# Attention distances: queries and their squares stacked on 128 rows, one product per head in column halves

## What is computed

```python
q, k, v = h @ Wq, h @ Wk, h @ Wv          # 8 heads of 64
k0, k1 = k - mu[0], k - mu[1]
d0 = -scale / 2.0 * sqdist(q, k0)         # sqdist = q.q + k.k - 2 q.k
d1 = -1.5 * scale * sqdist(q, k1)
prob = softmax(maximum(d0, d1), over the keys)
out = layernorm(h + (prob @ v) @ Wo)
```

## Time and profile before

| | |
|---|---|
| median of 3 runs | 2453.52 us (2449.77 to 2454.09) |
| profiled execution | 2452.1 us, span 2450.3 us |
| mean granted TensorE clock | 0.941 |
| attention stage in the trace | first work at 1489.3 us, last at 2054.5 us |

### The profile page before, as it was taken

How to read it: one execution, slowest core, us unless ns; L and a number is a source line. 1 busy time by engine, 2 the same in 40 slices (tenths; PEclk the granted TensorE clock), 3 DMA queues, 4 the chain that set the end, 5 groups by cost and what they waited for, 6 DMA issues and landing times. The chain is left out here.

```text
span 2450.3 us, 41718 instructions
## 1 busy us (share of the span) xinstructions
PE 2134.8 (87%) x14183; PEld 1496.8 (61%) x14183; DVE 1588.2 (65%) x3564; ACT 1230.3 (50%) x2063; POOL 915.0 (37%) x763
## 2 busy tenths in 40 slices
PE   5799999979998599999999997999999995776671
PEld 4567868855555466666666664777777774555450
DVE  4432333346777588888888875676767664666673
ACT  2334464344554367677667675555655562332330
POOL 0000000013443378777778772000000001786772
PEclk9999999989999699999999999999999996678995
DMA  7660010019920100000000000000000001214554
GB/s 262 245 245 18 27 34 11 1 43 419 420 117 2 69 1 1 0 0 0 0 0 0 0 1 20 1 0 0 0 0 0 0 1 45 83 43 122 165 154 154
DMA packets 64688, 165.46 MB, mean 68 GB/s; under 512 B 12310, under 2 KB 43460, under 8 KB 55084
## 3 DMA queue, kind: packets, MB, share of 16 engines
q1 hardware_dynamic: 51564, 148.42, 17.0%
q0 software_dynamic: 7104, 12.71, 1.5%
q10 hardware_dynamic: 5888, 2.62, 0.4%
HBM read 68.81 MB, written 96.86 MB: 68 GB/s over the span
## 5 line engine op out<-in xcount | busy, mean ns | idle before, releaser
L1261 POOL TENSOR_TENSOR c_both<-c_hid 128x512 f32<-128x512 f32 x384 | 491.6, 1287 | 144.5 <-ACT c_hid L1234 106.2
L1234 ACT ACTIVATE c_hid<-c_scaled,c_b 128x1024 f32<-128x1024 f32 x384 | 437.1, 1150 | 172.9 <-DVE c_scaled L1308 158.0
L1308 DVE TENSOR_TENSOR c_scaled<-c_p_h,c_shares 128x1024 f32<-128x1024 f32 x384 | 454.5, 1215 | 80.5 <-PE c_p_h L1177 79.5
L1182 PE MATMUL c_p_o<-c_both,c_w 128*128 128x512 f32 x768 | 390.8, 591 | 0.0
L1175 PE MATMUL c_p_h<-c_x_hi,c_w_hi 128*128 128x512 f32 x384 | 291.9, 760 | 2.6 <-DVE c_w_lo L1331 2.6
L624 POOL TENSOR_TENSOR d_ln_rstd<-d_ln_var,d_ln_power 128x2 f32<-128x2 f32 x48 | 33.4, 696 | 525.3 <-DVE d_ln_var L620 525.3
L240 POOL COPY a_work<-a_vec 128x64 f32<-128x64 f32 x4 | 1.2, 303 | 444.4 <-PE a_p_A L322 256.0
L1182 PEld LDWEIGHTS c_p_o<-c_both,c_w 128*128 128x128 f32 x768 | 144.3, 188 | 36.1 <-issue 2.2
L1176 PE MATMUL c_p_h<-c_x_lo,c_w_hi 128*128 128x512 f32 x384 | 152.6, 397 | 0.0
L1492 PEld LDWEIGHTS d_p_s<-d_kk,d_q_bd 128*128 128x128 f32 x768 | 123.9, 192 | 45.9 <-issue 45.9
L1177 PE MATMUL c_p_h<-c_x_hi,c_w_lo 128*128 128x512 f32 x384 | 151.9, 396 | 0.0
(11 more groups left out here) (331 smaller groups left out, 4658.6 us busy)
## 6 DMA issues: line engine op xcount, KB each, us to landing
slots<-b_blank SPq DMA_DIRECT2D x56, 1040.0 KB, 23.7
band_scratch<-a_work SPq DMA_DIRECT2D x16, 1024.0 KB, 5.7
a_work<-band_scratch SPq DMA_DIRECT2D x16, 1023.5 KB, 7.9
e_wb<-e_weights SPq DMA_DIRECT2D x63, 164.0 KB, 2.5
a_raw<-in_Wc SPq DMA_DIRECT2D x16, 512.0 KB, 3.6
e_xb<-slots SPq DMA_DIRECT2D x63, 130.0 KB, 2.2
e_yb<-e_again SPq DMA_DIRECT2D x12, 512.0 KB, 5.6
a_work<-in_x_tok SPq DMA_DIRECT2D x16, 256.0 KB, 8.2
```

The source lines that it names most:

```text
L1182: nc.tensor.matmul(p_o[s][:, 0:N], w2[:, q, :], both[q % SLOTS][:, :], start=(q == 0), stop=(q == NQ - 1)).then_inc(s_down, 1)
L1234: nc.scalar.activation(hid[q % SLOTS][:, :, :], scaled[q % SLOTS][:, :, :], ACT.Gelu, bias=b1[:, q:q + 1]).then_inc(s_ge, 1)
L1261: nc.gpsimd.tensor_tensor(both[q % SLOTS][:, :], hid[q % SLOTS][:, 0, :], hid[q % SLOTS][:, 1, :], ALU.add).then_inc(s_bo, 1)
L1308: v.tensor_tensor(scaled[q % SLOTS][:, :, :], p_h[q % SLOTS][:, 0:N].unsqueeze(1).to_broadcast([128, 2, N]), shares[s][:, :, :], ALU.mult) ...
```

## The change

- `q_bd`, `q_sq` and `q_rows` go. A new `q_two` has 128 rows per head: the head's 64 query rows on its own half and their squares on the other half.
- `kk` becomes `k_two`, per head: the head's keys (both kinds) on its own half, and on the other half the constants -0.5 and -1.5, written once by VectorE (`halves`).
- In `scores`, one product per head (128 rows in, 64 queries out) takes the place of two per head pair. Head `a` writes rows 64a to 64a+63 of `p_s`, so the two heads of a pair use the two column halves of the array. The product with `neg_half` stays.
- ScalarE's `queries` copies and squares each head from PSUM (four operations of 64 rows). A new ScalarE `keys` makes the keys of head 1 (two biased Identities, 64 rows) and both kinds of key squares from PSUM (two biased Squares, 128 rows, after a wait for VectorE's `keys`). `key_squares` goes.
- VectorE's `keys` makes only head 0's, on 64 rows. It takes over the second of the two value copies.
- The key projections wait for ScalarE's squares (`s_ksq`) where they waited for VectorE's keys (`s_k`).
- At the start GpSimd clears nothing, VectorE writes the constants and scaled means, and there are seven constant loads where there were eight.

The core of the diff:

```diff
@@ scores
-                pe.wait_ge(s_ksq, NT * g + t + 1)
-                pe.wait_ge(s_qsq, NHP * (g + 1))
+                pe.wait_ge(s_ksq, NHP * (g + 1))
+                pe.wait_ge(s_q, NHP * (g + 1))
+                if not exists(g - 2):
+                    pe.wait_ge(s_half, 2 * KINDS * (s + 1))
...
                     for hp in range(NHP):
-                        o = p_s[:, b, hp * 128:(hp + 1) * 128]
-                        nc.tensor.matmul(o, q_bd[s][:, hp, p, :], kk[s][:, p, hp, :, :].rearrange("p k j -> p (k j)"),
-                                         start=False, stop=False, skip_group_check=True)
-                        last = nc.tensor.matmul(o, q_sq[s][:, hp, p, :], q_rows[:, :], start=False, stop=hp == NHP - 1,
-                                                skip_group_check=True)
+                        for a in range(2):
+                            last = nc.tensor.matmul(p_s[64 * a:64 * a + 64, b, hp * 128:(hp + 1) * 128],
+                                                    q_two[s][:, hp, p, a, :],
+                                                    k_two[s][:, p, hp, a, :, :].rearrange("p k j -> p (k j)"),
+                                                    start=False, stop=hp == NHP - 1, skip_group_check=True)
@@ project and values
-                    pe.wait_ge(s_q if i % 2 == 0 else s_k, NHP * g + hp)
+                    pe.wait_ge(s_q if i % 2 == 0 else s_ksq, NHP * g + hp)
...
-                    pe.wait_ge(s_q if t == 0 else s_k, NHP * (g + 1))
+                    pe.wait_ge(s_q if t == 0 else s_ksq, NHP * (g + 1))
@@ ScalarE, queries and keys
                 for a in range(2):
-                    rows = slice(64 * a, 64 * a + 64)
-                    last = nc.scalar.copy(q_bd[s][rows, hp, :, 64 * a:64 * a + 64], by_position(p_p[0][rows, 0:M]))
+                    rows, other = slice(64 * a, 64 * a + 64), slice(64 - 64 * a, 128 - 64 * a)
+                    src = by_position(p_p[0][rows, 0:M])
+                    nc.scalar.copy(q_two[s][rows, hp, :, a, :], src)
+                    last = nc.scalar.activation(q_two[s][other, hp, :, a, :], src, ACT.Square)
                 last.then_inc(s_q, 1)
-                act.wait_ge(s_q, NHP * g + hp + 1)
-                nc.scalar.activation(q_sq[s][:, hp, :, :], q_bd[s][:, hp, :, :], ACT.Square).then_inc(s_qsq, 1)
...
+            def keys(g, s, hp):
+
+                if hp == 0 and exists(g - 2):
+                    act.wait_ge(s_s, NT * (g - 1))
+                act.wait_ge(s_proj, 10 * g + 2 * hp + 2)
                 for k in range(KINDS):
...
+                    nc.scalar.activation(k_two[s][64:128, :, hp, 1, k, :], by_position(p_p[1][64:128, 0:M]), ACT.Identity,
+                                         bias=mu_key[64:128, k, hp:hp + 1], scale=(1.0, 3.0)[k])
+                act.wait_ge(s_k, NHP * g + hp + 1)
+                for k in range(KINDS):
+                    last = nc.scalar.activation(k_sq[s][:, :, hp, k, :], by_position(p_p[1][:, 0:M]), ACT.Square,
+                                                bias=mu_sq[:, k, hp:hp + 1], scale=(1.0, 3.0 ** 0.5)[k])
                 last.then_inc(s_ksq, 1)
@@ ScalarE, values_out
-                for t in range(NT):
-                    act.wait_ge(s_proj, 10 * g + 9 + t)
-                    nc.scalar.copy(val[s][:, t, :], p_p[t][:, :]).then_inc(s_v, 1)
+                act.wait_ge(s_proj, 10 * g + 9)
+                nc.scalar.copy(val[s][:, 0, :], p_p[0][:, :]).then_inc(s_v, 1)
@@ ScalarE, body
                 def query(hp):
                     if ahead:
                         queries(g + 1, 1 - s, hp)
+                        keys(g + 1, 1 - s, hp)
@@ VectorE, keys and values_out
-                src = by_position(p_p[1][:, 0:M])
-                v.tensor_scalar(kk[s][:, :, hp, 0, :], src, mu[:, 0, hp:hp + 1], None, ALU.subtract)
-                v.tensor_scalar(kk[s][:, :, hp, 1, :], src, mu[:, 1, hp:hp + 1], 3.0, ALU.subtract, ALU.mult)\
+                src = by_position(p_p[1][0:64, 0:M])
+                v.tensor_scalar(k_two[s][0:64, :, hp, 0, 0, :], src, mu[0:64, 0, hp:hp + 1], None, ALU.subtract)
+                v.tensor_scalar(k_two[s][0:64, :, hp, 0, 1, :], src, mu[0:64, 1, hp:hp + 1], 3.0, ALU.subtract, ALU.mult)\
                     .then_inc(s_k, 1)
+
+            def values_out(g, s):
+                if exists(g - 2):
+                    dve.wait_ge(s_pv, NT * (g - 1))
+                dve.wait_ge(s_proj, 10 * g + 10)
+                v.tensor_copy(val[s][:, 1, :], p_p[1][:, :]).then_inc(s_v, 1)
@@ VectorE, body and start
                 if here:
                     probabilities(g, 1)
+                if ahead:
+                    values_out(g + 1, 1 - s)
                 if last:
                     ln2.statistics(dve, g - 1)
...
+            halves(0)
             dve.wait_ge(s_const, CONST)
+            v.tensor_scalar(mu_key[:, 0, :], mu[:, 0, :], -1.0, None, ALU.mult)
...
             for hp in range(NHP):
                 keys(0, 0, hp)
+            halves(1)
+            values_out(0, 0)
```

More of the change, by code:

```diff
@@ L1391, in phase_attention @@
         neg_half = sb("neg_half", [128, 128])
[L1392 removed]
+        mu_key = sb("mu_key", [128, KINDS, NHP])
+        mu_sq = sb("mu_sq", [128, KINDS, NHP])
         x_res = [sb(f"x_res{i}", [128, M]) for i in range(2)]
[L1395 to L1397 removed]
+        q_two = [sb(f"q_two{i}", [128, NHP, PB, 2, 64]) for i in range(2)]
+        k_two = [sb(f"k_two{i}", [128, PB, NHP, 2, KINDS, 64]) for i in range(2)]
         k_sq = [sb(f"k_sq{i}", [128, PB, NHP, KINDS, 64]) for i in range(2)]
@@ L1669, in body @@
                 query(3)
-                if ahead:
-                    key_squares(g + 1, 1 - s, 0)
                 if here:
@@ L1678, in body @@
                     vec_out(g, 0)
-                if ahead:
-                    key_squares(g + 1, 1 - s, 1)
-            act.wait_ge(s_set, 4)
             copy_x(0)
+            act.wait_ge(s_mu, 2)
             for hp in range(NHP):
                 queries(0, 0, hp)
-            for t in range(NT):
-                key_squares(0, 0, t)
+                keys(0, 0, hp)
             values_out(0, 0)
@@ L1694, in _ @@
             nc.gpsimd.memset(ln2.power[:, :], -0.5).then_inc(s_set, 1)
-            for q in q_bd:
-                nc.gpsimd.memset(q[:, :, :, :], 0.0).then_inc(s_set, 1)
-            pool.wait_ge(s_set, 4)
+            pool.wait_ge(s_set, 2)
             ln1.inverse_root(pool, 0)
@@ L1815, in body, with halves @@
                     ln2.normalise(dve, g - 1)
+            def halves(s):
+                for a in range(2):
+                    for k in range(KINDS):
+                        v.memset(k_two[s][64 - 64 * a:128 - 64 * a, :, :, a, k, :].rearrange("p b h j -> p (b h) j"),
+                                 (-0.5, -1.5)[k]).then_inc(s_half, 1)
             ln1.copy_in(dve, 0, columns(0), by_position)
```

20 lines of the change are left out of this document (6 added, 14 removed).

## The result

The changed kernel takes 2503.7 us (median of 4 runs, 2502.8 to 2505.7), beside 2453.3 us for the kernel before on the same chip: 1.0209 of it, with a 95% interval from 1.0194 to 1.0224. That is +50.4 us; the forecast was +41.5 (2495, range 2473 to 2522).

A forecast was written before the change was run, and what follows sets the result against it. TensorE was taken to bound the attention loop, with VectorE close behind. The new loop over three engines adds 22 x 1.57 = 34.5 us, start and end 7: 2453.5 + 41.5 = 2495, range 2473 to 2522.

The forecast's parts named there:

- rival A: TensorE's column halves run in turn, as the skill's weight-load rule would give: loop 25.4 us, 2525 in all; chance 0.06.
- Block and way back: On TensorE, one position's scores at 1.90 us, then 0.20 for returning to whole-array products.
- Rival C: TensorE stays the bound and its 2.3 us saving shows: 2441 to 2450 us; chance 0.05 faster.
- leg 4: ScalarE, from pair 0's Squares through `vec_out`, `exp`, pair 1's queries and keys to pair 2's key projection: 5.61 us.
- The ring: One attention step from pair 2's key projection to the next, over TensorE, VectorE and ScalarE: 24.04 us against 22.47.
- 1 project to output, residual: TensorE, from pair 2's key projection through one block, two projections, `norm_rows` and `output`: 5.84 us.
- 2 residual to distances: VectorE, from `residual` to ready for `distances`: 8.86 us today plus 0.61 for the added value copy, 9.47.
- 3 distances, shift, key: VectorE, `distances`, `shift` and the keys of pair 0: 3.12 us.
- rival B: TensorE's clock drops in the attention loop because of stalls, adding 0.4 to 0.8 us a step: 2504 to 2513; chance 0.12.
- its own +7: Attention stage's start and end: +6.2 to the first score product, +2 at step 1's layer norm, last step 1 shorter.
- a loop of 23.5 us: Low case for ScalarE's unknown prices: every such operation overlaps by 0.1 and bias is free; +27 in all, 2480.
- one of 24.9: High case for ScalarE's unknown prices: each such operation costs 0.05 to 0.1 more; +63 in all, 2516.

The follow-up runs named there:

- e1: Changed kernel with the score products issued head by head, all four pairs of one column half, then the other: ratio to the kernel before 1.0163.
- e4_fill: Changed kernel with four unread 128x256 products added on TensorE ahead of the key projection of pair 1: ratio to the kernel before 1.0126.
- e7: Changed kernel with the eight memsets of the constant halves on GpSimd instead of VectorE: ratio to the kernel before 1.0183.
- e2_key_early: Changed kernel with VectorE making the keys of pair 0 ahead of `shift(g, 0)`, not behind it: ratio to the kernel before 1.0010.
- e11_pool_alone: Changed kernel with only the key squares moved from ScalarE to GpSimd, with a second weight tile: ratio to the kernel before 1.0004.
- e5: Changed kernel with ScalarE's Squares of pair 0 moved behind `vec_out` and `exp(g, 0)`: ratio to the kernel before 1.0208.
- e10_pool_fixed: Changed kernel with key squares on GpSimd, squares products grouped per tile, both value copies on ScalarE: 2482.9 us beside 2517.9 for the kernel before.

## Why the prediction was right, and where it fell short

Its sign, its mechanism and most of its size held; it was 9 us short. That it came so close is in part luck, as two errors of opposite sign stand in the sum: the loop at full clock was put 6 to 7 us too long, and some 15 us of clock were left out. One of its own signs of being wrong came true, a granted clock under 0.95 from 1530 on: it was 0.92.

**The halves at once**: right. Sixteen records took 0.93 us without the tail against 0.89 forecast, and 1.42 with the heads in turn (e1). The rule beside rival A (the Trainium skill, "TensorE: Matmul & The Clock Gate", Part 3) doesn't hold for column halves here: by it no order of the heads could matter. Block and way back were forecast at 2.10 and took 2.01.

**ScalarE's prices**: right to 0.01 us each. Its lines and VectorE's, after (count, busy us, mean ns, idle):

```profile
L1612 ACT ACTIVATE d_k_sq<-d_p_p,d_mu_sq 128x256 f32<-128x256 f32 x154 | 64.7, 471 | 34.4 <-DVE d_k_two L1727 33.9
L1608 ACT ACTIVATE d_k_two<-d_p_p,d_mu_key 64x256 f32<-64x256 f32 x154 | 64.0, 463 | 1.9
L1599 ACT ACTIVATE d_q_two<-d_p_p 64x256 f32<-64x256 f32 x153 | 58.0, 379 | 1.8
L1598 ACT COPY d_q_two<-d_p_p 64x256 f32<-64x256 f32 x152 | 55.5, 365 | 11.8 <-PE d_p_p L1473 10.9
L1734 DVE COPY d_val<-d_p_p 128x512 f32<-128x512 f32 x19 | 13.0, 682 | 0.0
```

That is 0.47, 0.46, 0.38, 0.37 and 0.68 against 0.48, 0.473, 0.384, 0.367 and 0.693. The spacing of the four query operations is that of the earlier trace rows, with no overlap (1811.18, 1811.56, 1811.94, 1812.32). Rival C died here: the ten operations of leg 4 take 3.95 us, 0.40 each, not 0.26.

**The ring, leg by leg.** The changed kernel's legs, and those of e4_fill, which is the changed kernel at full clock:

| leg | forecast | e4 (clock 1.00) | changed kernel |
|---|---|---|---|
| 1 project to output, residual | 5.84 | 5.80 | 6.17 |
| 2 residual to distances | 9.47 | 9.45 | 9.45 |
| 3 distances, shift, key | 3.12 | 3.12 | 3.12 |
| 4 Squares to project | 5.61 | 5.41 | 5.55 |
| sum | 24.04 | 23.78 | 24.29 |

At full clock three legs are right to 0.04 and the fourth was put 0.20 too long: Squares and `vec_out` overlap what follows them and take 0.76 (1815.02 to 1815.75, and the wait ahead) and 0.51 in place of 0.90 and 0.56. So the working was good for 22 x 1.30 = 28.6 us of the loop and claimed 34.5 (e4's steps 1 to 22 take 521.2 us for 494.1, 27.1 more). With that and its own +7, the sum at full clock would have been 2489, 15 us under the measured time.

**The clock: the term that was missing.** The sum was made at full clock, and the clock stood aside as rival B with a chance of 0.12, on the ground that "work right after the stall has 1.5 us of slack". That ground didn't hold. The slack was the stall forecast before the projection of pair 2, 1.5 us (1.28 in e4); at the lower level the way from the key projection of pair 1 to the next query projection takes 4.04 us (1815.91 to 1819.95) where e4 takes 2.51 (1810.67 to 1813.18), 1.53 more. The slack is used up, leg 4 grows by 0.14, and the query bank of pair 2 comes late, for which ScalarE then waits 0.40 us; that returns as the 0.38 before the key projection of pair 3, in leg 1. With every sixth step at 25.5 the clock costs 0.67 a step, some 15 us in all: the price rival B was given (0.4 to 0.8). It wasn't a rival to the forecast but a part of it, since e4 shows that the stall before pair 1's key, forecast at 2.8 us in every step, is what brings it. The 2504 to 2513 of rival B came from adding that price to the loop's 34.5; the measured 2503.7 lies between 2495 and that.

**The predicted stalls**: 2.46 us before pair 1's key (2.8 forecast), ScalarE idle 1.46 (over 1), relu waiting 1.5 (under 2.0), `distances(g, 0)` not waiting: all seen. The stall before pair 2's key isn't there after, and is in e4: the lower clock hid it.

**The start.** ScalarE's longer list: +6.2 forecast, +6.4 measured, but not by its parts: ScalarE began 0.3 us later (1.3 forecast) and then took 14.2 us (13 forecast) for 8.1. Step 0 was put at +2 and came to +5.5. The memsets were sized right (0.91 each, 0.9 forecast), but e7 shows only 2.6 of it to be theirs, over steps 0 and 1. The cause of the rest isn't shown. It isn't mainly the ring, as e2_key_early, with the ring shortened, still has 26.5 us there for 27.2, while e11_pool_alone, with the memsets where they were and the Squares off ScalarE, has 21.4: that points at ScalarE's Squares. The tail was 1.9 shorter, 1 forecast. Together +10.0 for +7.

**Two bounds that don't add up.** By its own terms a loop of 23.5 us gives 22 x 1.03 + 7 = +30, not +27, and one of 24.9 gives +60, not +63. Neither moves the forecast.

## What to carry to other kernels

When a change takes work off the bound engine, draw the ring that the new waits close and add up its legs over all engines before counting the saving; here TensorE's shorter blocks (2.01 us for 2.65, 2.6 us a step) were real and worth nothing, since the Squares were put between a key bank and its release. A stall that such a sum forecasts on TensorE should be followed by a second sum with the work behind it at the lower clock. And where two ways run side by side, an edit that gives nothing isn't yet an edit without value: e5 gave nothing alone (24.46 us for 24.44) and 1.06 with the other way shortened.

## What the runs showed of the hardware that I hadn't expected

Useless products can be worth their time: 4 x 128x256 a step in a stall lifted the granted clock from 0.92 to 1.00 and took 0.67 us off a step of 24.4.

GpSimd's squares and some of VectorE's operations don't run side by side. `store_h` adds in SBUF; by tile, duration in ns (least, median, most), first in the changed kernel, then in e10_pool_fixed:

```profile
L1785 DVE TENSOR_TENSOR hT<-d_y,hT x18: 634/658/673, 1575.0 to 1991.2; 128x256 f32 x18
```

```profile
L1820 DVE TENSOR_TENSOR hT<-d_y,hT x21: 1206/1236/1283, 1566.2 to 1983.9; 128x256 f32 x20, 128x256 f32<-128x256 f32 x1
L1784 DVE TENSOR_SCALAR d_d_low<-d_d_min x48: 170/172/659, 1519.8 to 2005.3; 128x8 f32<-128x8 f32 x48
L1722 POOL TENSOR_TENSOR d_k_sq<-d_k_two x192: 1033/1038/1577, 1499.8 to 1989.5; 64x512 f32<-64x512 f32 x192
```

`store_h` takes 1.24 us for 0.66 while GpSimd's products run. The tiny operation of L1784 takes 0.17 where no product runs and 0.37 to 0.66 in the 23 cases of 48 in which one was under way at its start, and each time it ends 0.02 to 0.03 us behind that product:

```profile
1801.22 2.16 POOL L1722 TENSOR_TENSOR d_k_sq<-d_k_two 64x512 f32<-64x512 f32 x2 [0.16 <-DVE d_k_two L1762]
1802.96 0.45 DVE L1784 TENSOR_SCALAR d_d_low<-d_d_min 128x8 f32<-128x8 f32 x1
1803.44 0.69 DVE L1786 SCALAR_TENSOR_TENSOR d_dist<-d_dist,d_d_low 128x512 f32<-128x512 f32 x1
```

The products end at 1803.38, the tiny operation at 1803.41. It goes the other way too. GpSimd products that start while `store_h` or the last operation of `probabilities` is running take 1.34 to 1.57 us for 1.04. `shift` (L1786) is 0.69 in all 48 cases, but that shows no immunity: it met a product only once, had begun 0.02 us before it, and that product is the one of 1.58 us. VectorE's keys, which read PSUM, take 0.47 beside a product or without. In the profile the wait looks like a longer operation, not like a wait.

ScalarE operations in different row halves follow each other with no overlap (0.38 apart for 0.37 of duration), and two of the same kind and rows overlap by 0.1 us (0.83 for two Identities of 0.463). Half the rows cost the same as all of them (0.365 for the 64-row copies, 0.372 and 0.386 for the 128-row ones of `vec_out`).
